# Order of VectorE's table work, convolution pieces of block 0 one slot ahead, and y's fourth sum behind the tenth product

## The chip, the cores and the metric

The kernel runs on one core of one Trainium2 chip. The metric is the device time of one execution in microseconds, the median over several runs. Three runs of the kernel before gave 325.42, 325.68 and 325.95 us.

## What is computed

The input x is [128 batch, 32 channels, 512 positions] in fp32. A convolution kernel K is made from small parameters, the result is masked by a length per batch row, put through an FFN in emulated fp8, and added to x:

```python
dt  = exp(log_dt);  A = -exp(log_A_real) + 1j*A_imag;  dtA = A*dt[:, None]
Ct  = (C[...,0] + 1j*C[...,1]) * (exp(dtA) - 1) / A
K   = 2*real(einsum('hn,hnl->hl', Ct, exp(dtA[:, :, None]*arange(512))))   # 32 channels, 64 modes
y   = (causal convolution of x with K, along the 512 positions) + x*D[:, None]
y   = y * (arange(512) < length[batch])                   # mask
q   = lambda z, s: fp8(clip(z/s, -448, 448)) * s          # rounding to fp8 e4m3
g, u = q(y) @ gate_w.T, q(y) @ up_w.T                     # 512 -> 1376
out = x + q(silu(g)*u) @ down_w.T                         # 1376 -> 512
```

## The kernel before, in words

Everything is held as products of TensorE. The 32 channels are cut into 8 blocks of HB = 4 channels (NBLK = 8), so that a block has 4 * 128 = 512 tokens. For one channel the convolution is a product of a Toeplitz tile `toep[par][:, h]` (read from a padded copy of K in DRAM, `kpad_scratch`) with the transposed x in `xt[par][:, h]`, in four pieces ("distances" 0 to 3, of 512, 384, 256 and 128 columns, each an fp32 product that the trace shows as two matmuls). It lands in `y_ps[h % 2]`. `conv(g, par, half, h, distances)` issues some of these pieces for channel h of block g; the piece 0 waits until the bank is free (`ym_done`), the piece 2 is the last and releases `y_ready`.

From y_ps the chain for channel h goes over four VectorE and four ScalarE instructions: `mask_y` (VectorE, L825, writes ym), `scale_y` (ScalarE, L362 and L363, writes yv), `magnitude_y` (ScalarE, L370 and L373, writes yc), `sum_y` (VectorE, L833, writes yt), `round_y` (VectorE, L844, writes yq in bf16), `clip_y` (VectorE, L851, releases `yq_ready`). `round_y` reads what `sum_y` wrote and waits for it by a semaphore (`yt_done`).

The FFN of a block runs in CH = 11 slots, one for each chunk of 128 hidden rows (`slots` on each engine; slot c of block g has number n = 11 g + c). In slot c TensorE computes gate and up (L547, four matmuls each), then `beside` puts in pieces of the next blocks' convolution by a table, CONV_PLAN, and four matmuls of the block before's down projection (`down_part`, L503). Entries of CONV_PLAN are (blocks ahead, channel, distances) by slot. ScalarE takes silu of gate (L398). VectorE takes the product silu(gate)*up (`product`, L860). Two banks each hold gate and up, so TensorE's slot n waits for product n - 2 (`prod_done`). For each pair of chunks follow abs on ScalarE (`abs_prod`, L381, writes hc), `rounded_sum` (VectorE, L868, writes ht), `rounded` (L877, writes hq) and `clip` (L885). A product into a tile hv must wait until the `rounded_sum` that read it is done (`t_done`). hc, ht and hv have two tiles each.

The order on VectorE is written out by hand, by tables: MASK_PLAN, SUM_PLAN, ROUND_PLAN say in which slot y's steps for the next block stand, H_BEHIND and H_EVEN where `rounded` of each pair stands. Blocks 0, 1 and 6 go by H_BEHIND. In slot 8 VectorE runs product 8, rounded_sum of pair 3, sum_y of channel 3 and clip of pair 1, in this order, and in slot 9 product 9, round_y of channel 3 and clip_y of channel 3.

Slot 0 of a block is special: gate and up are computed for three channels first, then `beside`, then for the last channel, once its y is ready. Block 0 has a prologue instead (`by_channel(h)`, L508 to L518: gate and up of slots 0 and 1 for one channel at a time), with the convolution of block 1's channels 0 and 1 between. Its `beside` uses CONV_PLAN, skipping the entry (1, 1).

Ahead of this stands the making of K, in three groups of channels (K_GROUPS). For group i VectorE makes `turns` (three instructions), ScalarE takes sines (`waves(i)`), VectorE damps them (`decayed(i)`, L708) and forms coefficients (`g_of(i)`, L788 to L792), TensorE sums (`k_of(i)`, L450 and L454), the result is copied to krow (group 0 by VectorE, groups 1 and 2 by ScalarE's `copy_k(i)`, L344), and SyncE stores it to DRAM (`store_k`, L241). Toeplitz tiles are loaded from there: block 0's and block 1's channel by channel (`toep_first`), block 2's after group 2 is stored (L226). Four `mask` tables (L804 to L815) are made between these steps.

SyncE's queue then runs, in order: x and Toeplitz tiles of block 2, `copy_x(0, 0)` (1 MB of x copied to the output, DRAM to DRAM), `next_conv(3, 1)` (waits until all convolutions of block 1 are done, then loads block 3's x and Toeplitz tiles), `copy_x(1, 1)`, and a loop. GpSimd's queue loads the weights, wd last (L296, L298), then adds results to the output. TensorE waits for wd before block 1.

Of the kernel before, what the change touches and what calls it, by code (L numbers as in the profile page):

```python
# [25 lines left out]
ALU = mybir.AluOpType  # L26
# [52 lines left out]
def adaln_ffn_kernel(nc, xT, xn, params, scales, unit, stepped, wg_d, wu_d, wd_d, out):  # L79
# [4 lines left out]
    with ExitStack() as ctx:  # L84
# [127 lines left out]
        @block.sync  # L212
        def _(sp):
            sp.dma_start(prm[:], params).then_inc(params_in, 16)
            sp.dma_start(sl[:], scales).then_inc(scales_in, 16)
            sp.wait_ge(zeros_set, 1)

            sp.dma_start(bass.AP(kpad, 0, [[ROW, C], [1, PADK]]), zrow[:, 0:PADK]).then_inc(zeros_in, 16)
            sp.dma_start(one_by_one[:, 0], unit).then_inc(unit_in, 16)
            sp.dma_start(by_step, stepped).then_inc(unit_in, 16)  # L220

            def load_x_t(g, par):
                sp.dma_start(xt[par][:], xT[g]).then_inc(xt_in[par], 16)

            def load_toep(g, par):
                sp.dma_start(toep[par][:], toep_d[g]).then_inc(conv_in[par], 16)  # L226

            def copy_x(g, par):
                sp.dma_start(out[:, bass.ts(g, HB), :], xn[:, bass.ts(g, HB), :]).then_inc(copied[par], 16)

            load_x_t(0, 0)
            load_x_t(1, 1)

            def store_k(b):

                lo, n = 2 * K_GROUPS[b].start, 2 * (K_GROUPS[b].stop - K_GROUPS[b].start)
                if b:
                    sp.wait_ge(k_copied, 2 * b)
                else:
                    sp.wait_ge(k_first, 2)  # L240
                sp.dma_start(bass.AP(kpad, lo * ROW + PADK, [[KB, KA], [ROW, n], [1, KB]]),  # L241
                             krow[:, lo:lo + n, :]).then_inc(k_stored[b], 16)

            store_k(0)
            sp.wait_ge(zeros_in, 16)
            sp.wait_ge(k_stored[0], 16)
            for h in range(HB):
                sp.dma_start(toep[0][:, h], toep_d[0, :, h]).then_inc(toep_first[h], 16)
            store_k(1)
            sp.wait_ge(k_stored[1], 16)  # L250
            for h in range(HB):
                sp.dma_start(toep[1][:, h], toep_d[1, :, h]).then_inc(toep_first[HB + h], 16)
            store_k(2)

            def next_conv(g, par):
                at_least(sp, y_ready, HB * (g - 1))
                load_x_t(g, par)
                load_toep(g, par)

            sp.wait_ge(y_ready, HB)  # L260
            load_x_t(2, 0)
            sp.wait_ge(k_stored[2], 16)
            load_toep(2, 0)
            copy_x(0, 0)
            next_conv(3, 1)
            copy_x(1, 1)
            with sp.Fori(0, (NBLK - 4) // 2) as j:
                for par in range(2):
                    at_least(sp, added[par], 16 * (j + 1))
                    copy_x(2 * j + 2 + par, par)  # L270
                    next_conv(2 * j + 4 + par, par)
            sp.wait_ge(added[0], 16 * (NBLK // 2 - 1))
            copy_x(NBLK - 2, 0)
            sp.wait_ge(y_ready, HB * (NBLK - 1))
            sp.dma_start(xt[0][:], xn[:, HB * (NBLK - 1):HB * NBLK, :]).then_inc(xlast_in, 16)
            for t, part, cols in LAST_PARTS:
                sp.wait_ge(last_done, t + part + 1)
                sp.dma_start(out[:, HB * (NBLK - 1) + t, cols], xt[0][:, t, cols]).then_inc(stored, 16)
            sp.wait_ge(stored, 16 * len(LAST_PARTS))
# [38 lines left out]
        def _(act):  # L318
# [21 lines left out]
            def copy_k(i):  # L340

                for half in range(2):
                    act.wait_ge(k_ready, 2 * i + half + 1)
                    nc.scalar.copy(rows_of_k(i, half), k_in_bank(i, half)).then_inc(k_copied, 1)  # L344
# [67 lines left out]

            act.wait_ge(scales_ready, 1)
            for h in range(HB):
                if h:
                    scale_y(0, h)
                else:
                    cols = slice(0, L // 2)
                    act.wait_ge(ym_first, 1)
                    nc.scalar.activation(yv[0][:, 0, cols], ym[0][:, cols], ACT.Copy,  # L420
                                         scale=fac[:, D_GATE:D_GATE + 1]).then_inc(yv_first, 1)
                    nc.scalar.activation(yv[0][:, 1, cols], ym[0][:, cols], ACT.Copy,
                                         scale=fac[:, D_UP:D_UP + 1]).then_inc(yv_first, 1)
                    act.wait_ge(ym_done, 1)
                magnitude_y(0, h)
            copy_k(2)
            scale_y(1, 0)
            magnitude_y(1, 0)
            slots(0, 0, None, True, 2)
# [10 lines left out]
        def _(pe):  # L440
# [67 lines left out]
            def by_channel(h):  # L508

                pe.wait_ge(yq_ready, h + 1)  # L510
                cols = slice(h * B, (h + 1) * B)
                for c in range(2):
                    for ps, wt, version, ready in ((gate_ps, wg, 0, gate_ready), (up_ps, wu, 1, up_ready)):
                        for k in range(LB):
                            mm = nc.tensor.matmul(ps[c][:, cols], wt[:, k, c * P:(c + 1) * P],
                                                  yq[0][:, version, k, cols], start=(k == 0), stop=(k == LB - 1))
                        if h == HB - 1:
                            mm.then_inc(ready, 1)  # L518

            def beside(g, par, half, c, down, ahead):  # L520

                for step, h, distances in CONV_PLAN.get(c, ()):
                    if step <= ahead and (down or (step, h) != (1, 1)):
                        conv(g + step, (par + step) % 2, half + (1 if step == 2 else par), h, distances)
                if down:
                    down_part(g - 1, 1 - par, c)
# [44 lines left out]
            by_channel(1)  # L571
            conv(1, 1, 0, 1, [0, 1, 3, 2])
            by_channel(2)
            by_channel(3)
            pe.wait_ge(middle_in, 32)
            slots(0, 0, 0, False, 2)
# [28 lines left out]
        def _(dve):  # L605
# [3 lines left out]
            def did(ins):  # L609

                done[0] += 1
                ins.then_inc(chain, 1)
                return done[0]

            def after(tag):
                dve.wait_ge(chain, tag)
# [76 lines left out]
            def in_steps(ap):  # L693
                return ap.rearrange("p j (t m) -> p j t m", m=KA)
# [87 lines left out]

            def g_of(i):
                js = K_GROUPS[i]
                w = damped[0] if i == 0 else decayed(i)
                after(a)
                after(w)
                v.tensor_tensor(gu[:, js], wave[:, js, :, KB:], pair_by_j(s(38), js, KA), ALU.mult)  # L788
                w = did(v.tensor_tensor(gv[:, js], wave[:, js, :, KB:], pair_by_j(s(39), js, KA), ALU.mult))
                after(w)  # L790
                v.tensor_tensor(gk[:, js, 0], gu[:, js, 0], gv[:, js, 1], ALU.add)
                v.tensor_tensor(gk[:, js, 1], gv[:, js, 0], gu[:, js, 1], ALU.subtract).then_inc(g_ready, 1)  # L792
# [7 lines left out]
            for half in range(2):  # L800
                dve.wait_ge(k_ready, half + 1)
                v.tensor_copy(rows_of_k(0, half), k_in_bank(0, half)).then_inc(k_first, 1)
            after(last)
            v.tensor_scalar(mask[:, 0, :], lenf[:], cst[:, LEN0:LEN0 + 1], None, ALU.is_gt)  # L804
            after(w)
            v.tensor_tensor(turns[:, js], turns[:, js], whole[:, js], ALU.subtract).then_inc(turns_ready, 1)
            js = K_GROUPS[2]
            w = did(v.tensor_tensor(in_steps(turns[:, js]), tau_by_j(js), steps(js), ALU.mult))
            v.tensor_scalar(mask[:, 1, :], lenf[:], cst[:, LEN0 + 1:LEN0 + 2], None, ALU.is_gt)
            after(w)  # L810
            w = did(v.tensor_scalar(whole[:, js], turns[:, js], MAGIC, MAGIC, ALU.add, ALU.subtract))
            v.tensor_scalar(mask[:, 2, :], lenf[:], cst[:, LEN0 + 2:LEN0 + 3], None, ALU.is_gt)
            after(w)
            v.tensor_tensor(turns[:, js], turns[:, js], whole[:, js], ALU.subtract).then_inc(turns_ready, 1)
            v.tensor_scalar(mask[:, 3, :], lenf[:], cst[:, LEN0 + 3:LEN0 + 4], None, ALU.is_gt).then_inc(scales_ready, 1)  # L815
            g_of(1)
            g_of(2)
            dve.wait_ge(scales_ready, 1)

# [183 lines left out]

CONV_PLAN = {
# [5 lines left out]
MASK_PLAN = {0: 1, 3: 2, 5: 3}  # L1012
SCALE_PLAN = {0: (1, 0), 1: (1, 1), 4: (1, 2), 6: (1, 3)}
MAGNITUDE_PLAN = {1: (1, 0), 2: (1, 1), 5: (1, 2), 7: (1, 3)}
SUM_PLAN = {2: 0, 3: 1, 6: 2, 8: 3}
ROUND_PLAN = {4: 0, 5: 1, 7: 2, 9: 3}
H_BEHIND = {3: 0, 7: 1, 10: 2}
H_EVEN = {3: 0, 7: 1, 9: 2, 10: 3}
# [60 lines left out]
```

## Time and profile before

| | |
|---|---|
| median of 3 runs | 325.68 us |
| the profiled execution | 325.52 us, of which its span is 323.8 us |
| TensorE busy (matmul) | 310.2 us, 96% |
| VectorE busy | 303.2 us, 94% |
| ScalarE busy | 206.9 us, 64% |
| DMA | 38.38 MB, mean 119 GB/s |
| granted TensorE clock | 1.00 of full |

The profile is of one execution. 1.72 us of its time lie outside of its span. Times are microseconds from the start of the span. A line of the timeline gives start, duration, engine, source line, operation, what it wrote and read with its size, how many instructions are merged, and in brackets how long the engine was idle before it and what ended that. A VectorE instruction can start before the one ahead has ended, so distances between starts, not durations, add up to VectorE's time. Durations of matmuls are modelled and overlap likewise.

### The profile page before, as it was taken

To read this page: it belongs to the slowest core of one execution; us is meant where nothing else is said; L and a number is where in the kernel's file an instruction comes from. 1 tells how busy PE (TensorE), PEld (TensorE's weight loads), DVE (VectorE), ACT (ScalarE), POOL (GpSimd) and SP (SyncE) were. 2 spreads that over 40 slices of the span, in tenths; PEclk is the share of its full clock that TensorE was granted. 3 is DMA by queue.
4 is the path that set the end of the run, shared out by engine and by line. 5 is a ranking of instruction groups with operands and counts; after the bars stand their busy time and mean duration, and the time that the engine had idled before them with its cause. 6 is when DMAs were issued, how large, how long until landed. Compare 5 with 4: busy or idle time off the path is not lost.

```text
span 323.8 us, 4771 instructions
## 1 busy us (share of the span) xinstructions
PE 310.2 (96%) x1569; PEld 162.9 (50%) x1595; DVE 303.2 (94%) x464; ACT 206.9 (64%) x318; POOL 12.5 (4%) x20
## 2 busy tenths in 40 slices
PE   1999999999999999999999999999999999989996
PEld 1467554545455554555455454555455454534444
DVE  6999999999999999999998999989998999989784
ACT  4858788188755777486845868376863959364540
POOL 2031000000001000010001000010001000010010
PEclk9999999999999999999999999999999999999999
DMA  6879999300002690078202780067401650051028
GB/s 201 181 181 231 268 278 383 148 1 2 0 0 28 150 343 3 1 130 279 110 0 36 165 317 1 0 121 249 150 0 16 134 243 0 0 97 34 2 31 228
DMA packets 14014, 38.38 MB, mean 119 GB/s; under 512 B 1470, under 2 KB 6558, under 8 KB 11052
## 3 DMA queue, kind: packets, MB, share of 16 engines
q1 hardware_dynamic: 8412, 26.58, 23.2%
q0 software_dynamic: 5584, 11.57, 20.6%
q8 instruction: 10, 0.16, 0.2%
q14 instruction: 8, 0.07, 0.1%
HBM read 33.90 MB, written 15.81 MB: 154 GB/s over the span
## 4 chain that ended last, share of the span: by engine, by line
PE 72%; DVE 19%; issue 4%; ACT 4%; DMA 1%; DVEq 0%; ACTq 0%
PE gate_ps L547 19%; PE up_ps L547 18%; PE down_ps L503 17%; PE y_ps L489 15%; DVE hv L860 3%; DVE yq L844 3%; DVE yt L833 2%; DVE hq L877 2%; DVE ht L868 2%; PE y_ps L598 1%; DVE ym L825 1%; PE down_ps L598 1%; ACT hc L381 1%; DMA prm<-in_params 1%; DVE hq L885 1%
## 5 line engine op out<-in xcount | busy, mean ns | idle before, releaser
L398 ACT ACTIVATE sil<-gate_ps,fac 128x512 f32<-128x512 f32 (+1 forms) x88 | 59.6, 680 | 67.8 <-PE gate_ps L547 66.8
L547 PE MATMUL gate_ps<-yq,wg 128*128 128x512 bf16 (+3 forms) x365 | 88.2, 363 | 2.7 <-DVE hv L860 2.4
L547 PE MATMUL up_ps<-yq,wu 128*128 128x512 bf16 (+3 forms) x367 | 88.4, 363 | 0.3
L489 PE MATMUL y_ps<-xt,toep 128*128 128x512 f32 (+1 forms) x248 | 78.1, 434 | 0.0
L503 PE MATMUL down_ps<-wd,hq 128*128 128x512 bf16 (+1 forms) x295 | 76.8, 379 | 0.7
L860 DVE SCALAR_TENSOR_TENSOR hv<-up_ps,fac,sil 128x512 f32<-128x512 f32 (+1 forms) x88 | 65.5, 744 | 8.2 <-ACT sil L398 6.6
L381 ACT ACTIVATE hc<-hv 128x1024 f32<-128x1024 f32 (+1 forms) x48 | 47.0, 980 | 20.9 <-DVE hq L877 19.8
L547 PEld LDWEIGHTS gate_ps<-yq,wg 128*128 128x128 bf16 x372 | 35.6, 100 | 43.6 <-ACT sil L398 4.0
L489 PEld LDWEIGHTS y_ps<-xt,toep 128*128 128x128 f32 x248 | 45.9, 190 | 19.9 <-issue 2.4
L868 DVE SCALAR_TENSOR_TENSOR ht<-hc,hv 128x1024 f32<-128x1024 f32 (+1 forms) x48 | 54.1, 1127 | 1.9 <-ACT hc L381 1.9
L547 PEld LDWEIGHTS up_ps<-yq,wu 128*128 128x128 bf16 x372 | 36.3, 100 | 38.3
L877 DVE SCALAR_TENSOR_TENSOR hq<-hc,ht 128x1024 bf16<-128x1024 f32 (+1 forms) x48 | 53.8, 1126 | 0.3
L503 PEld LDWEIGHTS down_ps<-wd,hq 128*128 128x128 bf16 (+1 forms) x308 | 30.1, 98 | 37.9 <-issue 12.6
L844 DVE SCALAR_TENSOR_TENSOR yq<-yc,yt 128x1024 bf16<-128x1024 f32 x32 | 39.0, 1217 | 0.1
L833 DVE SCALAR_TENSOR_TENSOR yt<-yc,yv 128x1024 f32<-128x1024 f32 x31 | 37.7, 1217 | 0.0
L370 ACT ACTIVATE yc<-ym,fac 128x512 f32<-128x512 f32 x32 | 22.8, 713 | 2.9 <-DVE yq L844 2.9
L362 ACT ACTIVATE yv<-ym,fac 128x512 f32<-128x512 f32 x31 | 22.1, 712 | 3.2 <-DVE ym L825 3.2
L373 ACT ACTIVATE yc<-ym,fac 128x512 f32<-128x512 f32 x32 | 22.8, 712 | 0.0
L363 ACT ACTIVATE yv<-ym,fac 128x512 f32<-128x512 f32 x31 | 22.0, 709 | 0.0
L825 DVE TENSOR_TENSOR ym<-y_ps,mask 128x512 f32<-128x512 f32 x31 | 21.1, 681 | 0.0
L388 ACT ACTIVATE res<-down_ps,fac 128x512 f32<-128x512 f32 x28 | 19.0, 679 | 2.2 <-PE down_ps L503 2.1
L885 DVE TENSOR_SCALAR hq<-hq 128x1024 bf16<-128x1024 bf16 (+1 forms) x48 | 18.4, 397 | 0.3
(155 smaller groups left out, 118.1 us busy)
## 6 DMA issues: line engine op xcount, KB each, us to landing
xt<-in_xT SPq DMA_DIRECT2D x8, 1024.0 KB, 7.6
out<-in_x SPq DMA_DIRECT2D x7, 1024.0 KB, 5.6
out<-res POOLq DMA_DIRECT2D x7, 1024.0 KB, 7.8
toep<-kpad_scratch SPq DMA_DIRECT2D x6, 1024.0 KB, 10.0
toep<-kpad_scratch SPq DMA_DIRECT2D x8, 256.0 KB, 3.9
wd<-in_down POOLq DMA_DIRECT2D x1, 1280.0 KB, 21.3
xt<-in_x SPq DMA_DIRECT2D x1, 1024.0 KB, 7.3
out<-xt SPq DMA_DIRECT2D x3, 256.0 KB, 3.1
```

The source lines that it names most:

```text
L370: gate = nc.scalar.activation(yc[q][:, 0, :], ym[q][:], ACT.Abs, scale=fac[:, R_GATE:R_GATE + 1])
L381: nc.scalar.activation(hc[e % 2][0:w, 0:k], hv[e % 2][0:w, 0:k], ACT.Abs, scale=UP20).then_inc(abs_ready, 1)
L398: nc.scalar.activation(sil[b][0:w, :], gate_ps[b][0:w, :], ACT.Silu, scale=fac[0:w, S_GATE:S_GATE + 1]).then_inc(silu_done, 1)
L489: last = nc.tensor.matmul(y_ps[h % 2][:, d * P:L], toep[par][:, h, d * P:(d + 1) * P], xt[par][:, h, 0:L - d * P], start=(d == 0), stop=(d ...
L503: mm = nc.tensor.matmul(down_ps[t % 2][:], hq[par][0:w, k, t * P:(t + 1) * P], wd[0:w, k, :], start=(k == 0), stop=(k == CH - 1))
L547: mm = nc.tensor.matmul(ps[b][0:w, cols], wt[:, k, c * P:c * P + w], yq[par][:, version, k, cols], start=(k == 0), stop=(k == LB - 1))
L825: v.tensor_tensor(ym[q][:], y_ps[q][:], mask[:].rearrange("p k b -> p (k b)"), ALU.mult).then_inc(ym_done, 1)
L833: v.scalar_tensor_tensor(yt[q][:], yc[q][:], FLOOR, yv[q][:], ALU.max, ALU.add).then_inc(yt_done, 1)
L844: v.scalar_tensor_tensor(yq_of(par, h), yc[q][:].rearrange("p v (k b) -> p (v k) b", k=LB), FLOOR, yt[q][:].rearrange("p v (k b) -> p (v k ...
L860: v.scalar_tensor_tensor(hv[c // 2 % 2][0:w, c % 2], up_ps[b][0:w, :], fac[0:w, S_UP:S_UP + 1], sil[b][0:w, :], ALU.mult, ALU.mult).then_i ...
L868: v.scalar_tensor_tensor(ht[e % 2][0:w, 0:k], hc[e % 2][0:w, 0:k], FLOOR, hv[e % 2][0:w, 0:k], ALU.max, ALU.add).then_inc(t_done, 1)
L877: v.scalar_tensor_tensor(hq[par][0:w, 2 * e:2 * e + k, :], hc[e % 2][0:w, 0:k], FLOOR, ht[e % 2][0:w, 0:k], ALU.max, ALU.subtract, reverse ...
```

## The change

Five edits:

- SyncE: `next_conv(3, 1)` now stands ahead of `copy_x(0, 0)`.
- ScalarE: `copy_k(2)` moves from behind y's four channels of block 0 to ahead of the fourth one.
- TensorE: block 0 uses a table of its own, FIRST_PLAN, in which every piece stands one slot (for some: one entry) earlier. The first, `conv(1, 1, 0, 2, [0])`, moves out of slot 1 and into the prologue, between `by_channel(2)` and `by_channel(3)`.
- VectorE, tables: the `turns` of groups 1 and 2 are made without mask tables between, each instruction waiting for the one ahead; `decayed(1)` comes right after, then two masks, `g_of(1)`, two masks, `decayed(2)`, `g_of(2)`.
- VectorE, all blocks: SUM_PLAN puts `sum_y` of channel 3 in slot 9 instead of 8, so behind product 9 (the tenth), and right ahead of `round_y` of channel 3.

```diff
@@ sync
             load_toep(2, 0)
+            next_conv(3, 1)
             copy_x(0, 0)
-            next_conv(3, 1)
             copy_x(1, 1)
@@ scalar
             for h in range(HB):
+                if h == HB - 1:
+                    copy_k(2)
                 if h:
                     scale_y(0, h)
...
                 magnitude_y(0, h)
-            copy_k(2)
             scale_y(1, 0)
@@ tensor
-                for step, h, distances in CONV_PLAN.get(c, ()):
-                    if step <= ahead and (down or (step, h) != (1, 1)):
+                for step, h, distances in (CONV_PLAN if down else FIRST_PLAN).get(c, ()):
+                    if step <= ahead:
...
             by_channel(2)
+            conv(1, 1, 0, 2, [0])
             by_channel(3)
@@ vector
-                w = damped[0] if i == 0 else decayed(i)
+                w = damped[i]
...
-            after(last)
-            v.tensor_scalar(mask[:, 0, :], lenf[:], cst[:, LEN0:LEN0 + 1], None, ALU.is_gt)
             after(w)
             v.tensor_tensor(turns[:, js], turns[:, js], whole[:, js], ALU.subtract).then_inc(turns_ready, 1)
             js = K_GROUPS[2]
-            w = did(v.tensor_tensor(in_steps(turns[:, js]), tau_by_j(js), steps(js), ALU.mult))
+            link(v.tensor_tensor(in_steps(turns[:, js]), tau_by_j(js), steps(js), ALU.mult))
+            link(v.tensor_scalar(whole[:, js], turns[:, js], MAGIC, MAGIC, ALU.add, ALU.subtract))
+            v.tensor_tensor(turns[:, js], turns[:, js], whole[:, js], ALU.subtract).then_inc(turns_ready, 1)
+            damped.append(decayed(1))
+            after(last)
+            v.tensor_scalar(mask[:, 0, :], lenf[:], cst[:, LEN0:LEN0 + 1], None, ALU.is_gt)
             v.tensor_scalar(mask[:, 1, :], lenf[:], cst[:, LEN0 + 1:LEN0 + 2], None, ALU.is_gt)
-            after(w)
-            w = did(v.tensor_scalar(whole[:, js], turns[:, js], MAGIC, MAGIC, ALU.add, ALU.subtract))
+            g_of(1)
             v.tensor_scalar(mask[:, 2, :], lenf[:], cst[:, LEN0 + 2:LEN0 + 3], None, ALU.is_gt)
-            after(w)
-            v.tensor_tensor(turns[:, js], turns[:, js], whole[:, js], ALU.subtract).then_inc(turns_ready, 1)
             v.tensor_scalar(mask[:, 3, :], lenf[:], cst[:, LEN0 + 3:LEN0 + 4], None, ALU.is_gt).then_inc(scales_ready, 1)
-            g_of(1)
+            damped.append(decayed(2))
             g_of(2)
@@ plans
+FIRST_PLAN = {
+    6: [(2, 0, [0])], 7: [(2, 0, [1, 3])], 8: [(2, 0, [2]), (2, 1, [0])], 9: [(2, 1, [1, 3])],
+    1: [(1, 2, [1, 3])], 2: [(1, 2, [2]), (1, 3, [0])], 3: [(1, 3, [1, 3])], 4: [(1, 3, [2])],
+}
-SUM_PLAN = {2: 0, 3: 1, 6: 2, 8: 3}
+SUM_PLAN = {2: 0, 3: 1, 6: 2, 9: 3}
```

## Rows read from the trace of the kernel before

**Rows 1.** Page, chain of work that ended last: shares of the span by engine
```profile
PE 72%; DVE 19%; issue 4%; ACT 4%; DMA 1%; DVEq 0%; ACTq 0%
```

**Rows 2.** Windows: length, then busy us and instructions of each engine, clock, DMA share, GB/s
```profile
17.70:36.00 18.30, 17.96 (x192) 13.07 (x193) 17.48 (x27) 13.30 (x24) 4.42 (x6) 1.00 1.00 200
36.00:61.40 25.40, 24.43 (x112) 12.92 (x111) 25.10 (x32) 18.11 (x27) 0.00 (x0) 1.00 1.03 313
61.40:98.70 37.30, 37.03 (x167) 19.00 (x172) 36.66 (x48) 24.08 (x36) 0.00 (x0) 1.00 0.00 1
```

**Rows 3.** Timeline, from the first convolution to product 0 of block 0
```profile
17.77 0.73 PEld L560 LDWEIGHTS y_ps<-xt,toep 128*128 128x128 f32 x4 [0.18 <-DMA toep<-kpad_scratch]
...
34.93 0.39 PE L515 MATMUL up_ps<-yq,wu 128*128 128x128 bf16 x4
35.10 0.43 DVE L851 TENSOR_SCALAR yq<-yq 128x1024 bf16<-128x1024 bf16 x1
...
35.59 0.40 PE L515 MATMUL gate_ps<-yq,wg 128*128 128x128 bf16 x4 [0.27 <-DVE yq L851]
...
36.02 1.26 ACT L398 ACTIVATE sil<-gate_ps,fac 128x512 f32<-128x512 f32 x2 [0.75 <-PE gate_ps L515]
...
36.82 0.75 DVE L860 SCALAR_TENSOR_TENSOR hv<-up_ps,fac,sil 128x512 f32<-128x512 f32 x1
```

**Rows 4.** Timeline, TensorE, a convolution piece of distance 0 and its follower
```profile
66.21 1.02 PE L489 MATMUL y_ps<-xt,toep 128*128 128x512 f32 x2
67.07 1.03 PE L503 MATMUL down_ps<-wd,hq 128*128 128x512 bf16 x4
```

**Rows 5.** Timeline, VectorE in slots 8 and 9 of block 0, and TensorE behind
```profile
58.97 1.22 DVE L833 SCALAR_TENSOR_TENSOR yt<-yc,yv 128x1024 f32<-128x1024 f32 x1
...
60.11 0.42 DVE L885 TENSOR_SCALAR hq<-hq 128x1024 bf16<-128x1024 bf16 x1
60.45 0.74 DVE L860 SCALAR_TENSOR_TENSOR hv<-up_ps,fac,sil 128x512 f32<-128x512 f32 x1
61.11 1.21 DVE L844 SCALAR_TENSOR_TENSOR yq<-yc,yt 128x1024 bf16<-128x1024 f32 x1
61.43 0.82 PE L547 MATMUL gate_ps<-yq,wg 128*128 128x384 bf16 x4 [0.60 <-DVE hv L860]
```

**Rows 6.** Timeline, VectorE, a sum of y with its own rounding right behind
```profile
32.59 1.22 DVE L833 SCALAR_TENSOR_TENSOR yt<-yc,yv 128x1024 f32<-128x1024 f32 x1
...
33.84 1.23 DVE L844 SCALAR_TENSOR_TENSOR yq<-yc,yt 128x1024 bf16<-128x1024 f32 x1
```

**Rows 7.** Timeline, product 11 (block 1, slot 0) and TensorE's slot 2
```profile
65.76 1.23 DVE L868 SCALAR_TENSOR_TENSOR ht<-hc,hv 128x1024 f32<-128x1024 f32 x1 [0.26 <-ACT hc L381]
67.13 0.75 DVE L860 SCALAR_TENSOR_TENSOR hv<-up_ps,fac,sil 128x512 f32<-128x512 f32 x1
...
68.03 1.02 PE L547 MATMUL gate_ps<-yq,wg 128*128 128x512 bf16 x4
```

**Rows 8.** Timeline, product 16 (block 1, slot 5) and TensorE's slot 7
```profile
83.80 0.75 DVE L860 SCALAR_TENSOR_TENSOR hv<-up_ps,fac,sil 128x512 f32<-128x512 f32 x1
...
84.70 1.02 PE L547 MATMUL gate_ps<-yq,wg 128*128 128x512 bf16 x4
```

**Rows 9.** Timeline, product 77 (block 7, slot 0) and TensorE's slot 2
```profile
286.29 0.75 DVE L860 SCALAR_TENSOR_TENSOR hv<-up_ps,fac,sil 128x512 f32<-128x512 f32 x1
...
287.19 1.02 PE L547 MATMUL gate_ps<-yq,wg 128*128 128x512 bf16 x4 [1.01 <-DVE hv L860]
```

**Rows 10.** Timeline, ScalarE before y's channel 3, wd's tail, and copy_k(2)
```profile
28.92 0.72 ACT L362 ACTIVATE yv<-ym,fac 128x512 f32<-128x512 f32 x1 [0.77 <-DVE ym L825]
...
31.29 0.54 POOL L298 DMA_DIRECT2D wd<-in_down  x1
...
31.39 0.71 ACT L344 COPY hq<-down_ps 16x320 f32<-16x320 f32 x2
```

**Rows 11.** DMA issues between 10 and 60 us: KB, median us from issue to landing
```profile
wd<-in_down POOLq DMA_DIRECT2D x1, 96.0 KB, 26.2
```

## The prediction

> **What bounds the kernel now.** I read the chain of work that ended last first. TensorE has 72% of it, VectorE 19% [rows 1], and the rest is small. In order of time the chain is not mixed evenly. It runs on VectorE (with ScalarE) through the head and most of block 0, has short VectorE waits up to 85 us, then stays on TensorE up to about 262 us, and goes back to VectorE for the seam between blocks 6 and 7. So I read the windows next. From 17.7 to 36 us TensorE is busy 17.96 of 18.30 us; in block 0 VectorE is busy 25.10 of 25.40 us, and in block 1 both are full: 37.03 and 36.66 of 37.30 us [rows 2]. Then I read the timeline at each place where one engine hands the bound to the other. The reader is to see five regimes:
>
> - **A, 17.77 to 35.15 us: TensorE never pauses.** Its first convolution starts when the first Toeplitz tile lands, at 17.77; the last group of by_channel(2) starts at 34.93 and takes 0.22 us of issue [rows 3]. Only then does it wait, for y's channel 3: clip_y ends at 35.53 and by_channel(3) starts at 35.59 [rows 3]. 0.44 us of slack is all there is at that place.
> - **B, 36.82 to 84.55 us: VectorE never pauses**, but for gaps that its own chain makes. It starts with product 0, which waited for silu, which waited for by_channel(3): 35.59 gate, 36.02 silu, 36.82 product [rows 3]. TensorE follows it. Slot 2 of block 1 starts 0.15 us after product 11 ends (67.13 + 0.75 = 67.88, then 68.03) [rows 7], and slot 7 starts 0.15 us after product 16 ends (84.55, then 84.70) [rows 8].
> - **C, 84.70 to about 285 us: TensorE never pauses.** Products are done well ahead of the slot that wants them.
> - **D, blocks 6 to 7:** block 6 has fewer convolution pieces, VectorE has its full load and becomes the bound again. Slot 2 of block 7 starts at 287.19, after 1.01 us of idle, behind product 77 (286.29 + 0.75 = 287.04) [rows 9].
> - **E, the end:** TensorE again.
>
> A gain or a loss counts only if it moves the handover points: by_channel(3), products 11 and 16, product 77.
>
> **Part by part.**
>
> *The piece in the prologue (TensorE).* It comes out of slot 1, where TensorE waits for product 0 anyway, and goes in ahead of by_channel(3), at 34.93 + 0.22 = 35.15. A piece of distance 0 takes 67.07 - 66.21 = 0.86 us [rows 4]. It needs a bank and a tile that are both ready before that. So by_channel(3) starts at 35.15 + 0.86 = 36.01 instead of 35.59: +0.42, call it +0.43 with the change of data type. 0.43 of the piece lies in the old wait, 0.43 on the path. Silu and product 0 follow at the same distances: product 0 at 37.25. From there regime B is a sum of VectorE's own instructions, so products 11 and 16 come 0.43 later too. **+0.43 us.** Bounds: 0 (if VectorE's 0.30 us of idle in block 0 and the few tenths in block 1 [rows 2] took it all up) and 0.86 (the whole piece). I take 0.43: the idle spots that I find lie behind VectorE's own last instruction and ScalarE's answer to it, as before rounded_sum at 65.76 [rows 7], so they move with it.
>
> *The other pieces, one slot earlier (TensorE, block 0).* The first mask that depends on them runs in slot 3 and finds its bank done either way. TensorE gets slot 10 free of a piece. On the path: **0**. The cover is VectorE's backlog; without it a piece of 0.86 us would count. Its loads: block 2's tiles are wanted one slot earlier, and they are also loaded earlier (below).
>
> *The tables (VectorE, head).* Two masks leave the stretch ahead of group 2's turns, but each link now waits for its own result. I count turns ready some 0.3 us earlier, g_of(1) likewise, and decayed(2) at most 0.1 us, since four masks still stand ahead of it. All of that ends in regime A, where TensorE's start hangs on the Toeplitz tile of group 0, which no edit moves. y's channel 3 may be clipped 0.1 us sooner, but TensorE now comes there at 36.01, not 35.53. **0**; bounds -0.1 and 0.
>
> *copy_k(2) (ScalarE).* ScalarE idles 0.77 us ahead of the fourth channel's scale_y [rows 10], and where the two copies stood before they took 0.71 us [rows 10]. Behind them are queued channel 3's four ScalarE instructions; from 28.92, at 0.72 each, they end by 31.80, and the sum_y that wants them starts at 32.59 [rows 6]. **0**; if the copies came later than that by over 0.79 us, it would show in channel 3. SyncE's store of group 2, block 2's x and its Toeplitz load go out up to 3 us earlier.
>
> *SyncE's order.* copy_x(0, 0), 1 MB, now waits until block 1's convolutions are done; it is wanted only in slot 5 of block 1. Queued behind the new wait is nothing that is due sooner. wd's tail landed at 31.29 + 26.2 = 57.5 us [rows 10, 11], 4 us ahead of block 1's start at 61.43. DMA is full up to there [rows 2]; the copy leaves the time in which wd loads. **0.**
>
> *sum_y of channel 3 behind product 9 (VectorE).* Before, sum_y to clip is 60.11 - 58.97 = 1.14 us, a sum with an independent instruction behind it [rows 5]. Now round_y of the same channel is right behind the sum and must wait for it: 33.84 - 32.59 = 1.25 us [rows 6]. All else keeps its spacing, so what comes after slot 9 is 0.11 later, say 0.12. It happens in every block with a next one; it counts where VectorE is the bound: once in block 0 (product 11) and once in block 6 (product 77). **+0.12 and +0.12 us.** In blocks 1 to 5 TensorE covers it. The Trainium skill speaks against this term: "VectorE: DVE Perf Modes", section "The DRAIN you can't avoid", says that an instruction of VectorE waits for the pipe of the one before to empty with or without a semaphore, and that the semaphore costs nothing extra. By it the two terms would be 0 and the sum 325.95. The rows differ: 1.25 with the wait, 1.14 without.
>
> What the edit is good for: product 9 starts 1.14 earlier relative to VectorE's stream, at 60.45 + 0.43 - 1.14 = 59.74, ends at 60.48, and TensorE begins block 1 at about 60.6 instead of 61.43. But its next handover is product 11. That stands behind product 10, rounded of pair 2, abs on ScalarE, rounded_sum of pair 4; none of these gets shorter, and all come 0.43 + 0.12 = 0.55 later: product 11 at 67.68, slot 2 at 68.58. The lead of 0.8 us is waited away there, and more.
>
> **Sum.** 325.52 (the profiled execution: span 323.8 and 1.72 around it) + 0.43 + 0.12 + 0.12 = 326.19. The median of the runs is 0.16 above the profiled one, so on its scale 326.35. I say 326.3.
>
> **Rivals.**
>
> - *The lead holds (faster).* One mechanism: block 1 starts at 60.6, and product 11 doesn't hold TensorE. It would need VectorE to reach product 11 by 67.0 instead of 67.88 at its end. Then the kernel keeps 61.43 - 60.6 = 0.8: 325.52 - 0.8 = 324.7. For it speaks that VectorE before block 1 does the same work; against it that slot 2 followed product 11 at 0.15 us already [rows 7]. It decides when product 11 ends before 67.1. 10%.
> - *The delay is taken up.* VectorE's gaps in blocks 0 and 1 swallow the 0.43, and only the two 0.12 stay, or less: 325.8. For it: VectorE isn't at 100% in the windows [rows 2]. Against: the gaps sit in its own chain. 20%.
> - *The wait behind sum_y costs nothing*, so that only 0.43 stays: 325.95. Against it stand rows 6. 8%.
> - *DMA comes late (slower).* The earlier store and loads push wd's tail, or block 2's Toeplitz tiles, past the point of use; wd has 3.1 us left to the new start at 60.6. If it took 1 us more than that, 327.2. The Trainium skill, "DMA: Bandwidth & Descriptors", section "Issuing engines are not separate DMA queues", says that transfers of SyncE and GpSimd interleave on the same 16 engines. 7%.
> - *The tables do more than I see*, and the whole of y moves up 0.3 in the head. TensorE's unbroken run from 17.77 caps this at 0.1. It would give about 326.1, inside the forecast.
>
> **How the numbers follow.** Forecast (325.95 to 326.6 about 326.3) 55%, with the last rival in it; the others as above. The range holds 8 in 10: forecast, taken-up delay and the free wait, so 325.4 to 326.9, where the ends leave 0.3 for the scatter of medians. A measurement of this kernel can tell about 0.2%, 0.65 us, from no change. My sum is +0.67, right at that bound, so the forecast's 55% splits about in half. Slower by over 0.2%: 0.29 + 0.07 = 0.36. Faster: 0.10. Within: 0.26 + 0.20 + 0.08 = 0.54.
>
> **What would show it.** In the profile after: by_channel(3) at 36.0 without idle before it (step 1); product 0 at 37.25; VectorE's spacing from product 0 to product 8 as before; sum_y to round_y 1.25 in slot 9; block 1's first gate at 60.6; an idle of about 0.9 us before TensorE's slot 2 of block 1, at 68.6; slot 7 at 85.25; slot 2 of block 7 at 287.86. Wrong if slot 7 of block 1 starts at 84.7 or before: then VectorE's stream had room that I missed, or TensorE's prologue did.

## The result, and the profile after

The changed kernel takes 326.26 us (median of 20 runs, 326.04 to 326.80) where the kernel before took 325.59 in the same runs. The ratio is 1.0020, with a 95% interval of 1.0014 to 1.0026: slower by 0.67 us, which is clear of the scatter and small. The profiled execution of the changed kernel has a span of 324.6 us against 323.8.

The page first: busy time of the engines, then the chain of work that ended last, by engine.

```profile
PE 310.7 (96%) x1569; PEld 162.7 (50%) x1595; DVE 303.8 (94%) x464; ACT 206.4 (64%) x318; POOL 12.5 (4%) x20
...
PE 78%; DVE 16%; issue 4%; ACT 1%; DMA 1%; DVEq 0%; ACTq 0%
```

No engine has other work than before: the instruction counts are the same. In the chain TensorE has gained 6 per cent of the span, and VectorE and ScalarE have lost 3 each [rows 1]. The windows say where. Their columns are those of rows 2; the cut is at 60.60, where block 1 was forecast to start (it starts at 60.82).

```profile
17.70:36.00 18.30, 18.30 (x192) 13.06 (x191) 17.23 (x27) 13.44 (x24) 4.42 (x6) 1.00 1.01 214
36.00:60.60 24.60, 24.09 (x115) 13.02 (x115) 23.83 (x31) 18.00 (x27) 0.00 (x0) 1.00 1.04 312
60.60:98.70 38.10, 36.76 (x165) 18.52 (x169) 37.43 (x47) 24.09 (x36) 0.00 (x0) 1.00 0.00 2
```

In the prologue TensorE is now busy without any gap, 18.30 of 18.30 us. In the window of block 1 it has 1.34 us of gap where it had 0.27 [rows 2]; 0.22 of it lie ahead of the block's first gate, and 0.80 are one wait that is shown below. The timeline of the changed kernel at the first of these places answers rows 3:

```profile
34.99 0.39 PE L516 MATMUL up_ps<-yq,wu 128*128 128x128 bf16 x4
35.16 0.43 DVE L853 TENSOR_SCALAR yq<-yq 128x1024 bf16<-128x1024 bf16 x1
35.22 1.08 PE L490 MATMUL y_ps<-xt,toep 128*128 128x512 f32 x2
...
36.13 0.39 PE L516 MATMUL gate_ps<-yq,wg 128*128 128x128 bf16 x4
...
36.56 1.27 ACT L398 ACTIVATE sil<-gate_ps,fac 128x512 f32<-128x512 f32 x2 [1.23 <-PE gate_ps L516]
...
37.34 0.75 DVE L862 SCALAR_TENSOR_TENSOR hv<-up_ps,fac,sil 128x512 f32<-128x512 f32 x1 [0.62 <-ACT sil L398]
```

y's channel 3 is clipped at 35.59, but TensorE is in the moved piece and takes it up at 36.13. VectorE then idles 0.62 us before product 0, which starts 0.52 us later than before. Slot 9 of block 0, in answer to rows 5:

```profile
59.50 0.42 DVE L887 TENSOR_SCALAR hq<-hq 128x1024 bf16<-128x1024 bf16 x1
...
59.83 0.74 DVE L862 SCALAR_TENSOR_TENSOR hv<-up_ps,fac,sil 128x512 f32<-128x512 f32 x1
60.49 1.21 DVE L835 SCALAR_TENSOR_TENSOR yt<-yc,yv 128x1024 f32<-128x1024 f32 x1
60.82 0.82 PE L548 MATMUL gate_ps<-yq,wg 128*128 128x384 bf16 x4 [0.33 <-DVE hv L862]
...
61.74 1.22 DVE L846 SCALAR_TENSOR_TENSOR yq<-yc,yt 128x1024 bf16<-128x1024 f32 x1
```

Product 9 comes first and block 1 begins at 60.82 instead of 61.43. Sum to round is 1.25 us. And the three handovers, in answer to rows 7, 8 and 9:

```profile
67.77 0.75 DVE L862 SCALAR_TENSOR_TENSOR hv<-up_ps,fac,sil 128x512 f32<-128x512 f32 x1
...
68.66 1.02 PE L548 MATMUL gate_ps<-yq,wg 128*128 128x512 bf16 x4 [0.80 <-DVE hv L862]
```
```profile
84.45 0.75 DVE L862 SCALAR_TENSOR_TENSOR hv<-up_ps,fac,sil 128x512 f32<-128x512 f32 x1
...
85.34 1.02 PE L548 MATMUL gate_ps<-yq,wg 128*128 128x512 bf16 x4
```
```profile
287.05 0.75 DVE L862 SCALAR_TENSOR_TENSOR hv<-up_ps,fac,sil 128x512 f32<-128x512 f32 x1
...
287.95 1.02 PE L548 MATMUL gate_ps<-yq,wg 128*128 128x512 bf16 x4 [1.06 <-DVE hv L862]
```

TensorE, 0.6 us ahead at block 1's start, stands still for 0.80 us before slot 2, and is 0.63 behind from there. Slot 7 is 0.64 late, slot 2 of block 7 is 0.76 late.

**How the runs are compared below.** The differences are a few tenths, and medians of ten runs leave about as much open. The experiments ran in three groups, each with runs of the kernel before beside it, whose medians were 325.62, 325.61 and 325.56 us. A ratio isn't the quotient of the two medians, and differs from it by up to 0.0007. One of clip_between's twelve executions took 474.32 us at a granted clock of 0.665; the median counts it and the ratio doesn't. The profiles are sharper, if distances are taken inside one profile, between starts that hand the bound on. This table has them for the two kernels and all experiments, each distance the difference of two starts in the timeline of that kernel:

| kernel | first conv. | to by_channel(3) | to product 0 | product 0 to 11 | 11 to 16 | slot 7 to product 66 | 66 to 77 | span |
|---|---|---|---|---|---|---|---|---|
| before | 17.77 | 17.82 | 1.23 | 30.31 | 16.67 | 166.58 | 35.01 | 323.8 |
| changed | 17.83 | 18.30 | 1.21 | 30.43 | 16.68 | 166.59 | 35.12 | 324.6 |
| only_sum | 17.55 | 17.92 | 1.22 | 30.43 | 16.69 | 166.59 | 35.12 | 324.0 |
| only_pieces | 17.90 | 18.30 | 1.21 | 30.31 | 16.68 | 166.58 | 35.00 | 324.4 |
| sum_slot8 | 17.77 | 18.29 | 1.21 | 30.31 | 16.69 | 166.59 | 35.00 | 324.3 |
| piece_behind | 17.70 | 17.81 | 1.22 | 30.85 | 16.68 | 166.59 | 35.11 | 324.4 |
| clip_between | 17.98 | 18.30 | 1.21 | 30.31 | 16.68 | 166.59 | 35.00 | 324.5 |
| head_only | 18.15 | 17.81 | 1.23 | 30.31 | 16.68 | 166.59 | 35.00 | 324.2 |
| tables_only | 17.81 | 17.81 | 1.22 | 30.31 | 16.68 | 166.59 | 35.00 | 323.8 |
| queues_only | 17.57 | 17.96 | 1.22 | 30.32 | 16.69 | 166.59 | 35.00 | 323.8 |
| clip_y_later | 17.71 | 17.84 | 1.23 | 29.97 | 16.22 | 166.59 | 34.91 | 323.2 |
| no_waits_behind | 17.75 | 17.44 | 1.22 | 30.47 | 16.22 | 166.91 | 34.92 | 323.6 |
| clip_y_prologue | 17.64 | 17.57 | 1.23 | 29.92 | 16.23 | 166.59 | 34.91 | 322.8 |
| clip_y_prologue_sum9 | 17.87 | 17.44 | 1.22 | 29.92 | 16.22 | 166.59 | 34.91 | 322.9 |

The reader is to see that most columns repeat to 0.01 us between kernels, so that a difference of 0.1 is a finding. The one that doesn't is the first: the first convolution starts between 17.55 and 18.15. The second column hangs on it. Without the moved piece it is 17.81 to 17.84 where the first convolution starts at 17.70 or later, but 17.92 and 17.96 in only_sum and queues_only, where it starts at 17.55 and 17.57: there by_channel(3) waits longer for y's channel 3 (0.37 us of idle in only_sum, 0.27 in the kernel before), so part of an early start is waited away. With the piece TensorE is the bound, and the column is 18.29 or 18.30. In the last three rows an edit of the prologue shortens it.

### The profile page after: what moved, and what is told of

It is laid out like the page before. It is cut to its first block, busy times and chain, and to the rows that moved or that the text cites. A ratio compares the mean times of both kernels' runs of the same rounds, so it can differ in the third digit from the quotient of the medians.

```text
span 324.6 us, 4771 instructions
## 1 busy us (share of the span) xinstructions
PE 310.7 (96%) x1569; PEld 162.7 (50%) x1595; DVE 303.8 (94%) x464; ACT 206.4 (64%) x318; POOL 12.5 (4%) x20
## 4 chain that ended last, share of the span: by engine, by line
PE 78%; DVE 16%; issue 4%; ACT 1%; DMA 1%; DVEq 0%; ACTq 0%
PE y_ps L490 19%; PE gate_ps L548 18%; PE up_ps L548 17%; PE down_ps L504 17%; DVE hv L862 3%; DVE yq L846 3%; DVE hq L879 2%; DVE ht L870 2%; DVE yt L835 2%; PE y_ps L600 1%; PE y_ps L460 1%; PE down_ps L600 1%; ACT hc L381 1%; DVE hq L887 1%; DMA prm<-in_params 1%
```

## The experiments

### One edit alone, or one undone

**only_sum**: the kernel before with one entry changed.

```diff
-SUM_PLAN = {2: 0, 3: 1, 6: 2, 8: 3}
+SUM_PLAN = {2: 0, 3: 1, 6: 2, 9: 3}
```

> The kernel before with sum_y of channel 3 in slot 9 alone. Theory: +0.24 us, 0.12 at the seam of blocks 0 and 1 and 0.12 at that of 6 and 7, though block 1's first gate starts over 1 us sooner. Rival (the lead holds): 0.8 us faster. Rival (a page's rule, the wait is free): no change.

325.77 us; ratio 1.0003, interval 0.9994 to 1.0012. By the median alone this can't be told from no change. The distances can: product 0 to 11 is 30.43 instead of 30.31, product 66 to 77 is 35.12 instead of 35.01, all others stand. That is the +0.12 and +0.11. The lead is there and is waited away. Here too block 1 began early, and then:

```profile
67.12 0.75 DVE L860 SCALAR_TENSOR_TENSOR hv<-up_ps,fac,sil 128x512 f32<-128x512 f32 x1
...
68.02 1.02 PE L547 MATMUL gate_ps<-yq,wg 128*128 128x512 bf16 x4 [0.81 <-DVE hv L860]
```

0.81 us of idle before slot 2, right behind product 11. In blocks 1 to 5, where the sum moved as well, slot 7 to product 66 is unchanged at 166.59: TensorE covers it there.

**sum_slot8**: the changed kernel with that entry back at 8.

> The changed kernel with sum_y of channel 3 back in slot 8. Theory (the wait of round_y right behind its sum costs 0.12 at blocks 0 and 6): 0.24 us under the changed kernel, some 0.43 above before; block 1's first gate goes back from 60.8 to about 62. Rival (the wait costs nothing, and the early product 9 is of use): the same as the changed kernel or slower than it.

325.99 us; ratio 1.0010 (1.0001 to 1.0019). 30.31 and 35.00 are back; block 1's first gate starts at 61.89. Both as the theory has it.

**only_pieces**: the kernel before with FIRST_PLAN and the piece in the prologue.

> The kernel before with the convolution pieces alone: the first one in the prologue, all others of block 0 one slot ahead. Theory: 0.43 to 0.5 us above before. Rival (part of the loss is the tables' or the copy's): under 0.3 above.

326.04 us; ratio 1.0012 (1.0003 to 1.0021). First convolution to by_channel(3) is 18.30, as in the changed kernel, against 17.81 or 17.82 in the kernels without the piece whose first convolution starts at much the same time. So the piece costs 0.48 to 0.49 us (against only_sum and queues_only, with their early start, it would be 0.34 to 0.38, an estimate from the table), and the edit brings nothing back up to product 16 or later.

**piece_behind**: the changed kernel with only the first piece moved back behind by_channel(3).

```diff
             by_channel(2)
-            conv(1, 1, 0, 2, [0])
             by_channel(3)
...
 FIRST_PLAN = {
+    0: [(1, 2, [0])],
```

> The changed kernel with one edit undone: the piece of distance 0 of block 1's channel 2 stands behind by_channel(3) again instead of ahead of it; every other piece stays one slot ahead. Theory (the piece delays product 0 by 0.43 to 0.52 us, and VectorE carries that to product 16): product 0 back at 36.8 to 36.9, and the time 0.45 to 0.55 us under the changed kernel's, so 0.15 to 0.3 us above before. Rival (the piece's delay is taken up on the way, the loss is elsewhere): the time stays at the changed kernel's, 0.67 above before.

326.24 us; ratio 1.0012 (0.9999 to 1.0025). The expectation of the time, 0.15 to 0.3 us above before, was wrong. Product 0 is back at 36.73, but product 0 to 11 grew from 30.43 to 30.85. The piece was not free where I had put it: ahead of slot 2 TensorE then had it and also the pieces of distance 1 and 3, which FIRST_PLAN had moved there. Before product 0 let slot 2 go on, there was room for the one or the others, not for both: slot 2's gate starts at 38.20, 1.47 us behind product 0, where it was 1.11 in the two kernels. The lateness reached VectorE at product 5, by way of slot 4's gate (ScalarE's line is silu of slot 4, VectorE's is product 5):

```profile
44.87 0.69 ACT L398 ACTIVATE sil<-gate_ps,fac 128x512 f32<-128x512 f32 x1 [1.91 <-PE gate_ps L548]
```
```profile
48.33 0.75 DVE L861 SCALAR_TENSOR_TENSOR hv<-up_ps,fac,sil 128x512 f32<-128x512 f32 x1 [0.23 <-ACT sil L398]
```

From start to start, the clip ahead of product 5 and product 5 are 0.66 us apart where they were 0.33; that is most of the 0.42. So with the whole series one slot earlier the cost didn't go away in either place: it is 0.48 with the piece in the prologue and 0.42 with it in the slots. The third choice, the piece in the prologue and all others left where they were, wasn't run; nothing in the table suggests that it would be cheaper, since the 0.48 arises ahead of product 0.

### The wait of an instruction right behind the one it needs

**clip_between**: the changed kernel, sum still behind product 9, with an independent clip between sum and round.

```diff
+                    if c == 9 and ahead and 7 in plan:
+                        clip(PAIRS * g + plan[7], par, plan[7])
-                    if c - 1 in plan:
+                    if c - 1 in plan and not (c == 8 and ahead):
                         clip(PAIRS * g + plan[c - 1], par, plan[c - 1])
```

> The changed kernel with one move on VectorE: in slot 9 the clip of pair 1 stands between sum_y of channel 3 and its round_y, instead of ahead of product 9. The sum stays behind product 9. Theory (the loss of that edit is the wait of an instruction right behind the one it needs): sum to round is 1.48 us with a clip of 0.34 in it, 0.11 less in all, so product 0 to product 11 takes 30.31 as before instead of 30.43, and the time falls by 0.23 us under the changed kernel's. Rival (the loss is in the place of the sum): no fall.

325.94 us; ratio 1.0006 (0.9997 to 1.0015). VectorE in slot 9:

```profile
59.65 0.75 DVE L862 SCALAR_TENSOR_TENSOR hv<-up_ps,fac,sil 128x512 f32<-128x512 f32 x1
60.31 1.22 DVE L835 SCALAR_TENSOR_TENSOR yt<-yc,yv 128x1024 f32<-128x1024 f32 x1
61.44 0.42 DVE L887 TENSOR_SCALAR hq<-hq 128x1024 bf16<-128x1024 bf16 x1
61.78 1.22 DVE L846 SCALAR_TENSOR_TENSOR yq<-yc,yt 128x1024 bf16<-128x1024 f32 x1
```

Sum to clip 1.13, clip to round 0.34, 1.47 together, where the changed kernel needs 0.33 and 1.25, 1.58 together. 30.31 and 35.00 are back while product 9 stays ahead of the sum. The loss is the wait, not the place. The Trainium skill, "VectorE: DVE Perf Modes", section "The DRAIN you can't avoid", has measured no cost of the semaphore between chained copies, and in the same section adds: "A next op that is not held starts earlier". The trace agrees with the second and not with the first: here an instruction that waits for the one right ahead starts 0.11 to 0.12 us later than one that doesn't.

**clip_y_later**: the same wait taken out elsewhere. Every clip_y of the slots stands behind the next slot's product, in the kernel before.

```diff
                     product(n, m, par, c)
+                    if first and c == 2:
+                        clip_y(1, 1, 0)
+                    elif ahead and c - 1 in ROUND_PLAN and not (first and c == 5):
+                        clip_y(g + 1, 1 - par, ROUND_PLAN[c - 1])
...
                         round_y(g + 1, 1 - par, ROUND_PLAN[c])
-                        clip_y(g + 1, 1 - par, ROUND_PLAN[c])
```

> The kernel before with clip_y moved, in all slots, from right behind its round_y to behind the next slot's product, so that nothing on VectorE there waits for the instruction ahead of it. Theory (such a wait costs 0.11 and VectorE is the bound in block 0 up to slot 5 of block 1 and in block 6): 5 waits less up to product 16 and 4 less in block 6, so 0.5 us less by the first and up to 0.4 by the second, 324.7 to 325.1 in all. Rival (a wait right behind costs nothing): the time of before.

324.92 us; ratio 0.9978 (0.9968 to 0.9987): clearly faster than both kernels. Round to product is 1.13, product to clip 0.66:

```profile
49.28 1.22 DVE L844 SCALAR_TENSOR_TENSOR yq<-yc,yt 128x1024 bf16<-128x1024 f32 x1
50.41 0.75 DVE L860 SCALAR_TENSOR_TENSOR hv<-up_ps,fac,sil 128x512 f32<-128x512 f32 x1
51.07 0.42 DVE L851 TENSOR_SCALAR yq<-yq 128x1024 bf16<-128x1024 bf16 x1
```

Product 0 to 11 fell by 0.34: three of the moved clips save 0.12 to 0.13 each, and the fourth, in slot 1, was no use, because product 2 then came before its silu and waited 0.18 us. Product 11 to 16 fell by 0.45, but only 0.11 of that is a wait saved. The other 0.34 is the clip itself, which stood ahead of product 16 and now stands behind it. Slot 7 gained less than product 16 (16.67 + 0.90 became 16.22 + 1.16, 0.19 us), since TensorE is the bound there now. In block 6 only 0.10 was left of the four waits; what else holds product 77 there is open.

### What the edits of the head do

**head_only**: the changed kernel without pieces and without the sum's move.

> The changed kernel without its convolution pieces and without its sum_y: only the table order, copy_k(2) one channel sooner, and SyncE's order are left of the change. Theory (all of it ends ahead of or beside TensorE's unbroken run): the time of before, within 0.1 us; k_of(1) starts when TensorE's warm-up products end, at 16.8 to 17.2, though its coefficients are ready 0.3 us sooner. Rival (the rest of the loss of the changed kernel is here): 0.2 us or more above before. Rival (the tables help): 0.2 or more under it.

326.01 us; ratio 1.0007 (0.9998 to 1.0016). Its median looked like a loss of 0.4 that no step of mine had. In the profile all distances are those of before, and only the first convolution is late, by 0.38 us, at 18.15, which is all of the 0.4 between the spans (this is the weight load ahead of it):

```profile
18.14 0.73 PEld L561 LDWEIGHTS y_ps<-xt,toep 128*128 128x128 f32 x4 [0.58 <-DMA toep<-kpad_scratch]
```

So the two halves were run apart.

**tables_only** and **queues_only**: the table order alone, and copy_k(2) with SyncE's order alone, each on the kernel before.

> The kernel before with VectorE's new table order alone. The run of all three edits of the head had a median 0.40 above before, with its first convolution at 18.15 us in the profile after 0.49 us of waiting for the first Toeplitz tile. Theory (that tile lands at 17.5 to 18.1 us by chance, in kernels with and without the edits): within 0.15 us of before. Rival (the table order does it): 0.3 to 0.4 above before.

> The kernel before with copy_k(2) ahead of y's channel 3 and SyncE's new order alone, so the rest of the head's edits. Both act after 28 us, later than the first convolution. Theory: within 0.15 us of before; p0 to p11 30.31. Rival (the loss of the head's edits is here, by ScalarE or by wd's loading): 0.3 to 0.4 above before, and then a wait of TensorE before block 1 or of VectorE for ScalarE in the prologue.

325.59 us, ratio 0.9996 (0.9987 to 1.0005), and 325.80 us, ratio 1.0005 (0.9997 to 1.0014), both with a span of 323.8 in the profile. Neither shows the 0.4, and all distances behind product 0 are those of before. The tables do what they say, to no use: k_of(1) starts at 16.56, 0.34 sooner than before, and then TensorE waits for the same tile as ever:

```profile
16.56 0.52 PEld L450 LDWEIGHTS gate_ps<-res,hq 64*16 64x16 f32 x32 [0.56 <-DVE hq L792]
17.13 0.11 PEld L454 LDWEIGHTS gate_ps<-prm 1*16 1x16 f32 x4
17.80 0.73 PEld L560 LDWEIGHTS y_ps<-xt,toep 128*128 128x128 f32 x4 [0.56 <-DMA toep<-kpad_scratch]
```

So the loss of the profiled execution is a late first tile. The eleven executions of head_only spread from 325.26 to 326.38 us, and the fastest is under the fastest of the kernel before beside it (325.39), so the edits don't cost 0.4 us each time. Whether its high median was chance, or the two halves together make a late tile more frequent, stays open.

### Towards a faster version

**no_waits_behind**: clip_y_later, with the prologue's steps interleaved and product 3 ahead of the first rounded.

```diff
             mask_y(0, 3)
-            clip_y(0, 0, 1)
             sum_y(0, 2)
+            clip_y(0, 0, 1)
             round_y(0, 0, 2)
-            clip_y(0, 0, 2)
             mask_y(1, 0)
             sum_y(0, 3)
+            clip_y(0, 0, 2)
             round_y(0, 0, 3)
...
+                    product(n, m, par, c)
                     if first and c == 3:
                         rounded(m - 1, g, par, 0)
-                    product(n, m, par, c)
```

> A version meant to be the faster one, from the kernel before: clip_y behind the next product as in the run beside this one; in the prologue y's sum, clip and round of neighbouring channels interleaved, so that by_channel(3) can start 0.3 us sooner; product 3 ahead of the first rounded. Theory: 0.3 for the prologue, 0.66 in blocks 0 and 1, up to 0.4 in block 6: 324.3 to 324.6. TensorE's unbroken run from the first convolution caps the prologue's part at 0.44. Rival (TensorE takes over as the bound in block 0): no more than the run beside this one.

325.28 us; ratio 0.9988 (0.9979 to 0.9997), worse than the run beside it. by_channel(3) did come 0.4 sooner (17.44). But product 3 now stands in front of its silu:

```profile
42.49 0.75 DVE L860 SCALAR_TENSOR_TENSOR hv<-up_ps,fac,sil 128x512 f32<-128x512 f32 x1 [0.53 <-ACT sil L398]
```

A wait of 0.12 was traded for one of 0.53. The profile lost another 0.32 us far behind, in slot 7 of block 2 (the 166.91 of the table): a convolution piece starts at 123.36 there, after 0.55 us in which the weight loads stood idle for no other engine that the profile names. No other kernel's profile has it, and its cause is open.

**clip_y_prologue**: that swap undone, and block 0's first clip_y left in its place.

> The faster version, mended: clip_y behind the next product in all slots but slot 1 of block 0 (there product 2 waited 0.18 us for its silu instead), the prologue's sums, clips and rounds interleaved, product 3 behind the first rounded again (ahead of it, it waited 0.53 us for its silu). Theory: product 0 at 36.4, product 0 to 11 in 29.97, so 0.3 to 0.35 us under the version with clip_y moved alone (324.92): 324.6. Rival (TensorE is the bound by then): no gain over 324.9.

324.48 us in five executions; ratio 0.9962 (0.9949 to 0.9975). With the next run it is the fastest, 1.1 us under the kernel before and 1.8 under the changed one. Of the 1.05 us by which product 77 comes sooner than before, 0.13 are the first convolution's start, for which no edit accounts; 0.25 are the prologue, 0.39 product 0 to 11, 0.19 the way from there to slot 7, and 0.10 block 6.

**clip_y_prologue_sum9**: the same with the sum behind product 9, a clip between sum and round.

> The version beside it, with sum_y of channel 3 behind product 9 and the clip of pair 1 between sum and round. Theory (TensorE's earlier start of block 1 is worth something once VectorE isn't the bound up to slot 7): with clip_y moved, product 16 was done 0.26 us before slot 7 started, so up to 0.3 us under the version beside it: 324.3. Rival (it is still waited away): the same as that.

324.54 us; ratio 0.9969 (0.9959 to 0.9979), no gain over the run beside it: the expectation missed by 0.2. Block 1 starts at 60.30 instead of 60.81, and TensorE waits again:

```profile
67.35 1.02 PE L547 MATMUL gate_ps<-yq,wg 128*128 128x512 bf16 x4 [0.40 <-DVE hv L860]
```

I had looked at slot 7, where product 16 was early, and not at slot 2, where product 11 is still the last to come, with or without the edit.

## Why the prediction was right, point by point

- **The time.** 326.3 was forecast, 326.26 was measured. The forecast case was the one that happened; the chances by sign leaned to "within 0.2%", and the measured 0.20% lies on that line. That the two numbers agree to 0.04 us is luck in part. The forecast started from 325.68, the median of three runs, and twenty gave 325.59; and its terms add up to 0.67, where the profiles have product 77 later by 0.76.
- **The piece in the prologue**, +0.43. Right in mechanism, short in size: 0.48 to 0.49 in four profiles with the piece. The piece itself took from 35.22 to 36.13, 0.91 us instead of 0.86. The 0.05 is not shown to have one cause, but it seems to go with the products of 128 columns ahead of the piece rather than with what follows: in piece_behind three pieces of together 1024 columns stand behind such products and ahead of a gate of 512 columns, and take 1.78 us where twice 0.86 would be 1.72. The first convolution was 0.06 late besides. Silu to product took 0.02 less. Together product 0 came 0.52 later.
- **No absorption in block 0.** The rival that VectorE's gaps take the delay up fell: product 0 to 11 is 30.43, of which 30.31 are the old distance, and 11 to 16 is unchanged. So none of the few tenths of idle in rows 2 could take up any of the delay.
- **The wait behind sum_y**, +0.12 twice. 0.12 and 0.11, in the changed kernel and in only_sum, and gone in clip_between. The rival by the Trainium skill's rule (325.95) fell with it.
- **The lead at block 1.** Forecast: gate at 60.6, waited away before slot 2, at 68.58. It was 60.82, and 68.66 after 0.80 us of idle. The lead was 0.6 us and not 0.8: product 0 came 0.09 later than forecast, and the forecast let the gate start 0.12 us behind product 9's end, where it starts 0.24 or 0.25 behind in both kernels (61.43 after 61.19 in rows 5). The faster rival (324.7) fell because product 11 had no slack, as rows 7 showed.
- **The other pieces, one slot earlier**, 0. Right as part of the whole, but the cover was smaller than "VectorE's backlog" lets one think. The price without it was put at a whole piece, 0.86. piece_behind showed how thin the cover is: one piece more in slot 1 and 0.42 us are lost at product 5.
- **The tables**, 0. Right; and the reason was half of it. The coefficients were ready 0.3 us sooner, as worked out. In the changed kernel k_of(1) still started later than before, at 17.07 instead of 16.90, behind TensorE's warm-up products, which the prediction had left out. And in this profile the first convolution doesn't wait for its tile, as regime A has it; it starts right behind k_of(1), with no idle ahead of it.
- **copy_k(2)**, 0. It ran at 28.20 for 0.73 us, and scale_y came at 28.98, 0.06 later than before, which is the shift of everything there.
- **SyncE's order and DMA**, 0. wd's tail was issued at 30.88 and landed 24.3 us later, at 55.2, which is 5.6 us ahead of block 1's first gate. The slower rival had nothing to stand on: wd was in time, and products 0 to 8 of block 0 keep their distances, so no tile of block 2 held them up.

```profile
30.88 0.54 POOL L298 DMA_DIRECT2D wd<-in_down  x1
```
```profile
wd<-in_down POOLq DMA_DIRECT2D x1, 96.0 KB, 24.3
```

The sum by measured terms: 0.06 + 0.48 - 0.02 to product 0, then 0.12 and 0.11, is 0.75, against 0.76 at product 77, 0.8 between the two spans and 0.67 between the medians. The 0.06 of the first convolution is within what it varies by.

## What to carry to other kernels

Ask of an earlier start which handover comes next: here TensorE began a block 0.6 us sooner and gave it back two slots later, at a product whose chain had not become shorter. Work moved out of an idle slot costs its full length less the slack at its new place, and everything moved along with it eats the cover of the others. Where an engine's own stream is the bound, look for instructions that wait for the one right ahead and put an independent one between; moving such clips, in the slots and in the prologue, gained 1.1 us where the whole change lost 0.67, but an instruction moved up must not land ahead of its input.

## What the runs showed of the hardware

**A wait for the instruction right ahead costs VectorE 0.11 to 0.12 us.** Sum to an independent instruction: 1.13 or 1.14. Sum to the round that needs it: 1.25. Round to clip_y is 1.24 to 1.26 with the wait, and round to an independent product 1.13.

**The start of the first convolution varies by 0.6 us** between profiles, 17.55 to 18.15, with no edit that explains it: among the five kernels that share the changed kernel's head it is 17.70 to 18.15. In some it waits for the first Toeplitz tile (0.58 us in head_only), in others it starts right behind k_of(1), which waits for its coefficients (only_sum) or for TensorE's 14 warm-up products (the changed kernel). These start every 0.43 us at first and every 0.2 us later, and the switch doesn't come at the same product. Windows over the warm-ups of the kernel before, then of the changed one (length, busy us of matmuls with their count, granted clock, DMA share, GB/s):

```profile
14.40:15.40 1.00, 1.00 (x4) 1.00 0.03 12
15.40:16.40 1.00, 1.00 (x7) 1.00 0.72 180
```
```profile
14.40:15.40 1.00, 1.00 (x4) 1.00 0.09 12
15.40:16.40 1.00, 1.00 (x6) 1.00 0.85 162
```

The second window has one product fewer, and the series ends 0.17 us later, which is how k_of(1) came to start later in the changed kernel though its input was earlier. The granted clock reads 1.00 in all four windows, so the column doesn't show this.
